# Convolution units of an attention kernel in fewer, longer blocks, one group on another bank, and four VectorE steps placed otherwise

## Time and profile before

| | before |
|---|---|
| median of 3 runs | 521.07 us (520.21 to 521.3) |
| the profiled execution's own time | 521.39 us |
| its span, first to last instruction | 519.6 us, mean granted clock 0.983 |
| TensorE busy | 482.6 us, 93% |
| VectorE busy | 353.4 us, 68% |
| ScalarE busy | 263.6 us, 51% |
| GpSimd busy | 137.0 us, 26% |
| DMA | 13.18 MB |

### The profile page before, as it was taken

The page is one execution under the profiler, slowest core; times in us unless marked ns, Lnnn a source line. Parts: engine busy times, 40 slices in busy tenths (PEclk is TensorE's granted clock), DMA queues, the critical chain, the costliest instruction groups (busy, mean ns, idle before and its releaser), DMA issues.

```text
span 519.6 us, 10741 instructions
## 1 busy us (share of the span) xinstructions
PE 482.6 (93%) x3838; PEld 386.1 (74%) x3838; DVE 353.4 (68%) x895; ACT 263.6 (51%) x654; POOL 137.0 (26%) x161
## 2 busy tenths in 40 slices
PE   8798999989999999999999999999988998788895
PEld 7685876668687768777776887677676798788885
DVE  1528847895778678686967786786476345575995
ACT  3233576664646454555546464544524514984540
POOL 5320574271013102210410231021111112504662
PEclk9889999999999999999999999999997999998999
DMA  6000111000000000000000000000000000005111
GB/s 220 21 20 3 47 45 50 18 23 22 1 20 22 1 1 20 20 0 0 20 20 0 20 0 0 1 22 1 1 20 1 1 22 2 0 1 163 42 60 61
DMA packets 9488, 13.18 MB, mean 25 GB/s; under 512 B 496, under 2 KB 8816, under 8 KB 9328
## 3 DMA queue, kind: packets, MB, share of 16 engines
q1 hardware_dynamic: 9456, 12.76, 7.4%
HBM read 8.56 MB, written 4.19 MB: 25 GB/s over the span
## 4 chain that ended last, share of the span: by engine, by line
PE 63%; DVE 19%; ACT 7%; issue 6%; POOL 2%; DMA 1%; DVEq 0%; ACTq 0%
PE bank L1204 7%; PE bank L1206 5%; PE bank L1205 5%; PE bank L1405 5%; PE bank L1379 5%; PE bank L1323 4%; PE bank L1211 4%; PE bank L1355 3%; PE bank L1377 3%; DVE even L897 2%; PE bank L1433 2%; PE bank L1392 2%; ACT x L803 2%; PE bank L1228 2%; PE bank L1420 1%
## 5 line engine op out<-in xcount | busy, mean ns | idle before, releaser
L1204 PE MATMUL bank<-win,w_hi 128*128 128x256 f32 x384 | 120.8, 315 | 8.3 <-DVE v L1173 2.8
L1206 PE MATMUL bank<-win,w_lo 128*128 128x256 f32 x384 | 108.4, 282 | 0.0
L1205 PE MATMUL bank<-win,w_hi 128*128 128x256 f32 x384 | 108.3, 282 | 0.0
L745 ACT ACTIVATE prob<-bank 128x512 f32<-128x512 f32 x128 | 69.5, 597 | 72.7 <-PE bank L1377 72.0
L997 DVE TENSOR_REDUCE nmax<-bank 128x2 f32<-128x512 f32 x128 | 85.3, 684 | 21.8 <-PE bank L1355 21.4
L1204 PEld LDWEIGHTS bank<-win,w_hi 128*128 128x128 f32 x384 | 72.6, 189 | 19.9 <-issue 5.2
L1205 PEld LDWEIGHTS bank<-win,w_hi 128*128 128x128 f32 x384 | 72.9, 190 | 0.5
L1206 PEld LDWEIGHTS bank<-win,w_lo 128*128 128x128 f32 x384 | 72.7, 189 | 0.0
L522 POOL TENSOR_TENSOR first<-first 128x256 f32<-128x256 f32 x24 | 17.7, 738 | 165.0 <-ACT first L634 165.0
L1211 PE MATMUL bank<-ones_r 128*128 128x256 f32 x316 | 56.7, 321 | 1.1 <-DVE ones_r L851 1.1
L1211 PEld LDWEIGHTS bank<-ones_r 128*128 128x128 f32 x316 | 46.2, 212 | 5.8 <-issue 1.5
(11 more groups left out here) (237 smaller groups left out, 929.4 us busy)
## 6 DMA issues: line engine op xcount, KB each, us to landing
w_stage<-convs SPq DMA_DIRECT2D x4, 576.0 KB, 3.7
x_in<-x SPq DMA_DIRECT2D x8, 256.0 KB, 2.7
out<-x_pair SPq DMA_DIRECT2D x8, 256.0 KB, 2.2
q<-out SPq DMA_DIRECT2D x1, 2048.0 KB, 8.2
out<-v SPq DMA_DIRECT2D x8, 256.0 KB, 2.1
cst<-small SPq DMA_DIRECT2D x1, 1708.0 KB, 9.3
cst<-small SPq DMA_DIRECT2D x1, 253.5 KB, 3.1
```

The costliest lines, as they stand in the source:

```text
L745: act.activation(prob[:, x // 4 % 2, x % 4, :, :], bank[ST_BANK[x % 2]][:, :], ACT.Exp, scale=L2_SCALE).then_inc(st_exp, 1)
L1204: mm(dst, hi, x_hi, start=(row == 0), stop=False)
L1205: mm(dst, hi, x_lo, start=False, stop=False)
L1206: return mm(dst, lo, x_hi, start=False, stop=(row == KH - 1))
```

## The change

It has these parts:

- CONV_NOW and CONV_NEXT: the same 18 and 18 units in other slots. The blocks of CONV_NEXT are 6, 6 and 6 units in slots 0, 3 and 6 (before 3, 3, 3, 3, 1, 3, 2 in slots 0, 1, 3, 5, 6, 7, 8). Those of CONV_NOW are 3, 3, 3, 3, 3, 1, 2 in slots 13, 15, 17, 19, 21, 22, 23 (before 2, 1, 3, 3, 1, 2, 3, 1, 2 in slots 13, 14, 15, 17, 18, 19, 21, 22, 23). So group 3 ends in slot 0, group 4 in slot 3, group 5 in slot 6 (before 1, 5, 8), and group 4's `first_copy` stands in slot 3 (before 5).
- JOIN_SLOTS keeps the joins of groups 2/3 and 4/5 in slots 2 and 9, where they were.
- Group 4 goes to ST_BANK[0] (bank 3) for all pairs but the last two. It waits for k's first low part, group 5 waits for the join of group 3, and the first transposed scores wait for group 4's copy.
- VectorE: both of k's low parts in slot 1 (before slots 3 and 4), the gate in slot 11 (before 6), and the low part of the second image's convolution input in slot 12 (before on GpSimd in slot 11).
- ScalarE: the copy of v in slot 2 (before 3).

```diff
-DVE_SLOTS = {..., "e_min": 5, "gate": 6, "att0_inv": 7, "logit1": 9, "att1_n": 12, ...
+DVE_SLOTS = {..., "e_min": 5, "att0_inv": 7, "logit1": 9, "gate": 11, "att1_n": 12, ...
-CONV_NOW = (0, 0, 0, 0, 0, 0, 0, 0, 0, 0, 0, 0, 0, 2, 1, 3, 0, 3, 1, 2, 0, 3, 1, 2)
-CONV_NEXT = (3, 3, 0, 3, 0, 3, 1, 3, 2, 0, 0, 0, 0, 0, 0, 0, 0, 0, 0, 0, 0, 0, 0, 0)
+CONV_NOW = (0, 0, 0, 0, 0, 0, 0, 0, 0, 0, 0, 0, 0, 3, 0, 3, 0, 3, 0, 3, 0, 3, 1, 2)
+CONV_NEXT = (6, 0, 0, 6, 0, 0, 6, 0, 0, 0, 0, 0, 0, 0, 0, 0, 0, 0, 0, 0, 0, 0, 0, 0)
+JOIN_SLOTS = {1: SLOTS + 2, 2: SLOTS + 9}
-    joined = {min(done[2 * w + 1] + 1, last): w for w in range(3) if done[2 * w + 1] is not None}
+    joined = {max(min(done[2 * w + 1] + 1, last), JOIN_SLOTS.get(w, 0)): w for w in range(3) ...}
-K_LOW_SLOTS, V_SLOT, HEADS_SLOT, PROJECT_SLOT, ONES_SLOT = (3, 4), 3, 4, 5, 5
+K_LOW_SLOT, V_SLOT, HEADS_SLOT, PROJECT_SLOT, ONES_SLOT = 1, 2, 4, 5, 5
         def conv_bank(j, g):
...
+            if g == 4 and not (isinstance(j, int) and j > PAIRS - 3):
+                return ST_BANK[0]
         # GpSimd's slots
-                    if s == LOW_SLOTS[1] and not (isinstance(j, int) and j == 0):
-                        window_low(j - 1, 1)
         # VectorE's slots
-                    if s in K_LOW_SLOTS:
-                        qk_low_parts(j, "k", (K_LOW_SLOTS.index(s),))
+                    if s == K_LOW_SLOT:
+                        qk_low_parts(j, "k")
-                    if s == LOW_SLOTS[0] and before:
-                        window_low(j - 1, 0)
+                    if s in LOW_SLOTS and before:
+                        window_low(j - 1, LOW_SLOTS.index(s))
         # TensorE: scores_t_pair, n == 0
                     pe.wait_ge(k_rows, 2 * j + 2)
+                    after(pe, first_copied, 3 * (j - 1))
         # TensorE: convolve
+                        elif conv_bank(j, g) == ST_BANK[0]:
+                            pe.wait_ge(qk_low, 4 * (j + 2) + QUADS + 1)
+                        elif conv_bank(j, g - 1) == ST_BANK[0]:
+                            pe.wait_ge(joined, 3 * j + 2)
```

More of the change, by code:

```diff
@@ L67 @@
              "hid0": 13, "filt": 13, "z0": 14, "red": 19}
-DVE_SLOTS = {"n2m": 1, "xh": 3, "xht": 5, "e_min": 5, "gate": 6, "att0_inv": 7, "logit1": 9, "att1_n": 12, "post_att": 14,
+DVE_SLOTS = {"n2m": 1, "xh": 3, "xht": 5, "e_min": 5, "att0_inv": 7, "logit1": 9, "gate": 11, "att1_n": 12, "post_att": 14,
              "se": 16, "x2": 16, "x1": 17, "gvar": 17, "xn": 19, "taps0": 20, "taps1": 21, "taps2": 22}
@@ L85, in conv_events @@
     summed = {min(done[2 * w] + 1, last): w for w in range(3) if done[2 * w] is not None}
-    joined = {min(done[2 * w + 1] + 1, last): w for w in range(3) if done[2 * w + 1] is not None}
+    joined = {max(min(done[2 * w + 1] + 1, last), JOIN_SLOTS.get(w, 0)): w for w in range(3) if done[2 * w + 1] is not None}
     return copied, summed, joined
@@ L511, in residual @@
                                    proj_bias[:, :].to_broadcast([P, PX]), ALU.add).then_inc(x2_res_done, 1)
[L513 to L517, removed]
             def first_sum(j, w):
```

## The result

The changed kernel is slower by 0.6%. The medians of 20 executions each are 525.66 and 521.58 us, and the ratio, taken without the slow executions (527.46, 528.03 and one of 866.34 us at full clock, whose cause isn't known), is 1.0062 (95% interval 1.0041 to 1.0083). The forecast was 524.5 against 521.07, a ratio of 1.0066. The size came out right, but by luck: the loop passes took 3.6 us less than forecast, the clock fell in two passes where the sum had nothing for it, and these errors made up for each other, as the passes show.

A forecast was written before the change was run, and what follows sets the result against it. TensorE's own queue was taken to bound a loop pass, nearly without waits. Four loop passes +4.15, pair 6 -0.7, pair 7 -0.6, pair 1 -0.5, pair 0 +1.1 gave +3.45: 524.5 us against 521.07, range 519.7 to 526.5.

The forecast's parts named there:

- the waits at z1, at slots 8 and 10 and at dot1: Signs: TensorE waits about 0.9 us at z1, 0.5 at slot 8, a few tenths at slot 10, over 1 at pair 0's dot1.
- the loop pass of 48.4: Sign: each of four loop passes takes 48.4 us instead of 47.4, +1.04 (bounds +0.6 and +1.3).
- z1's wait in the loop: Loop pass, slots 3 to 4: TensorE stands still 0.97 us for hid1's relu, behind first_copy and sum_x on ScalarE.
- The small waits that go: Loop pass, slots 0 to 8: waits of group 4 (0.16), group 5 (0.20) and slot 8's maxima (0.23) vanish.
- Merging in slots 0 to 7: Loop pass, slots 0 to 7: fewer, longer convolution blocks save 0.05 us of entry tolls.
- rival 1: All passes: each of 31 removed blocks saves 0.20 us, 4.6 less than forecast, 519.9 us; chance 0.20.
- Slots 8 to 12: Loop pass: VectorE decides, removing slot 8's block gains nothing, the added low part and gate cost +0.2 us (0 to +0.4).
- Slots 13 to 23: Loop pass: the blocks of slots 14 and 18 go, saving 0.20 us of tolls (0.09 and 0.11).
- Pair 0: First pass: k's low parts delay n2m, rn, weights and b_signed, so dot1 comes 1.1 us later (0 to +1.4).
- Pair 6: Pass outside the loop, no sum_x: larger waits go, -0.55 up to slot 8 and -0.15 behind, together -0.7 us.
- Rival 3: Clock falls in a further pass as pair 6 comes to resemble pair 7; costs up to 3.3 us, 527.8; chance 0.13.
- Pairs 1 and 7: Pair 1: CONV_NOW -0.2 and earlier maxima 0.3, so -0.5 us; pair 7: waits in slots 3 and 6 go, -0.6.

The follow-up runs named there:

- experiment 7: Changed kernel with sum_x moved from slot 3 to slot 5 of ScalarE's list, behind z1; ratio 0.9951 to the kernel before.
- experiment 8: Kernel before with the new CONV_NOW alone, CONV_NEXT and all else as before; 517.25 us, ratio 0.993 to the kernel before.
- experiment 4: Kernel before with one edit, both of k's low parts in slot 1 of VectorE; ratio 1.0062 to the kernel before.
- experiment 5: Changed kernel with 14 matmuls that nobody reads ahead of dot1 in pair 0; ratio 0.9997 to the kernel before.
- experiment 9: Changed kernel with unread matmuls, 14 ahead of dot1 in pair 0 and nine in pair 6; 521.2 us, ratio 0.9978 to the kernel before.
- experiment 3: Changed kernel with the blocks and banks of before, so only the VectorE and ScalarE places changed; ratio 1.0072 to the kernel before.
- 10: Changed kernel with n2m in slot 0, sum_x in slot 5 and nine unread matmuls in pair 6; 514.9 us, ratio 0.9887 to the kernel before.
- 11: Changed kernel with n2m in slot 0, sum_x in slot 5, pair 6's filler, and three CONV_NEXT units back in slot 8; 510.4 us, ratio 0.978.
- 2: Changed kernel with k's low parts back in slots 3 and 4 of VectorE; ratio 1.0338 to the kernel before.
- 6: Changed kernel with n2m in slot 0 of VectorE's list, ahead of k's low parts; 522.8 us, ratio 1.0036 to the kernel before.
- 1: Kernel before with the new blocks, join slots and group 4's bank alone; 539.7 us, ratio 1.036 to the kernel before.

## Why the prediction was right in size, and what in it was wrong

Of the signs named for it, the waits at z1, at slots 8 and 10 and at dot1 came; the loop pass of 48.4 did not, it was 47.57.

**z1's wait in the loop, forecast +0.97:** measured 1.77 - 0.94 = +0.83, and experiment 7 gives back 0.82. The step was right; two terms of its sum were a little long: the copy starts 0.19 after the next instruction of TensorE (247.48 to 247.67) and not 0.28, and from the relu's end to z1 it is 0.05 and not 0.09.

**The small waits that go, forecast -0.59:** about -1.04. Group 4's wait was 0.40 and not 0.16: the transposes ahead of it take 0.41 to the block's start in the changed kernel, 0.81 before. A row's idle time counts from the end of the record before, which is modelled, and so comes out too short, by 0.24 us here. The same holds for the maxima of slot 8, whose 0.23 was 0.45. The distance between starts, where the same pair stands elsewhere without a wait, was in the trace.

**Merging in slots 0 to 7, forecast 0.05:** about 0. v to scores takes 0.99 (0.81 to a block), pout to xht 0.44 (0.25 to a block), and what the blocks save goes there. Here the toll does move to the neighbours, and rival 1, for these slots, is wrong.

**Slots 8 to 12, forecast +0.2:** +0.56. VectorE decides there, as forecast: 0.65 and 0.49 us of distance at the two places, and 0.28 more at the block of slot 13 for the second low part.

**Slots 13 to 23, forecast -0.20:** -0.96 in the changed kernel, -0.88 with CONV_NOW alone (experiment 8). This is the step that failed. I priced it by the toll of a block's entry alone. What experiment 8 shows in its place: merging the blocks of slots 13 and 14 gave 0.20, z0 behind 32-row matmuls in place of a block 0.31, and slot 18 gave 0.37, of which 0.25 is the wait for VectorE's h_t that nine matmuls now hide. In the changed kernel the block of slot 13, which starts after a wait for VectorE, takes 1.27 and not 1.34. What is left for the tolls, 0.20 and 0.12 for the two blocks, is near the 0.20 of rival 1 in slot 14 and near my 0.11 in slot 18; more than half of the gain was in neither account, and in slots 0 to 7 rival 1's 0.2 for each block is not there.

The Trainium skill's TensorEngine Tiling (Array Packing), section Key Properties, says that a change of the tiling mode drains the engine. The rows agree in slot 14, where a block between 32-row scores and the 16-row z0 went and 0.20 and 0.31 us with it, and in slots 0 to 7, where the blocks that went stood next to 128-row products and their going saved nothing; how long a drain takes no run here tells apart.

So a loop pass grew by 0.13 and not by 1.04: four passes, 3.6 us less than forecast.

**Pair 0, forecast +1.1:** +5.57 in the profile, of which 1.2 are the wait (experiment 4) and 4.6 the clock behind it (experiment 5); the two are from different executions and add up to 0.2 too much. The wait was found from the order of n2m, rn and the weights, and was right in size; that it would let the clock fall I had said only of pair 6. This is the term that made up for the loop.

**Pair 6, forecast -0.7:** +1.96, of which the clock is 3.1: without the stretch it takes 43.99 (experiment 9) and 43.97 (experiment 7), so -1.1 by itself. Rival 3's outcome came true there, 6.8 us at half clock and 3.1 lost, beside the forecast. Its reason isn't shown: experiment 3 has the old blocks, slot 8's among them, and had a stretch of 3.4 us in pair 6 too. Whether the waits of pair 6 bring the stretch is open: with the filler it was gone in all three kernels profiled (experiments 9, 10 and 11), but without it there was one in the changed kernel and in experiments 2, 3, 5 and 6 and none in 1 and 7, and the changed kernel and experiment 7 have the same waits there (0.6, 0.5, 0.4 and 0.2 us) and differ in this pass by their timing only.

**Pairs 1 and 7, forecast -0.5 and -0.6:** -0.9 and, with all behind it, -0.3.

The two kernels' times vary more than their passes do, and the mean clock goes with them: the changed kernel's was 0.97 in ten of its executions, which took 525.5 to 528.0, 0.973 to 0.976 in four (524.1 to 524.6), and 0.977 to 0.986 in five, which took 519.6 to 522.7. The ratio of 1.006 is a mean over these.

## What to carry to other kernels

When a block of work is moved, follow the instructions that other engines tie to its end: here one copy that came two slots earlier in ScalarE's in-order queue cost 0.8 us a pass, and putting the sums that it pushed back two slots later turned a loss into a gain. Put fill work where an engine waits for another one's chain: three units back in slot 8 were worth 0.7 us a pass. And test the parts of a change one by one: the new CONV_NOW alone took 3.3 us off the median, and the rest of the change hid that. And where a wait is added to a busy TensorE, price the clock behind it apart from the wait: here the wait was 1.2 us of the pass and the clock 4.6.

## What the hardware showed that I had not expected

A wait of 1.9 us on TensorE was followed by 10.2 us at half clock in the changed kernel's profile; 14 matmuls without a reader in that wait kept the clock at full. A wait of 1.8 us in experiment 4 was not followed by any. The same kernel has executions 4 to 6 us apart, with a mean clock of 0.97 in the long ones and about 0.98 in the short ones. And a 16-row matmul issued behind eight 32-row ones and four more can have its start recorded among them and add nothing to the time (0.91 us with it and without it), where behind a 128-row block it took 0.31.
